# Order and waits of the DMA queue's loads where one Fourier layer ends and the next begins

## The reference, cut to what matters

```python
h = layer_norm(x @ fc0_w + fc0_b, ln0_g, ln0_b)
for i in range(4):
    x_ft = rfft2(h)
    out_ft[:, :, :12, :12]  = einsum('bixy,ioxy->boxy', x_ft[:, :, :12, :12],  w1[i])
    out_ft[:, :, -12:, :12] = einsum('bixy,ioxy->boxy', x_ft[:, :, -12:, :12], w2[i])
    h = layer_norm(irfft2(out_ft) + einsum('bchw,oc->bohw', h, conv_w[i]) + conv_b[i], ...)
    if i < 3: h = gelu(h)
```

## Time and profile before

| | |
|---|---|
| Runs | 3142.08, 3146.17 and 3292.08 us, median 3146.17 |
| Profiled execution | 3139.24 us |
| Its span, first to last instruction | 3137.6 us |
| PE busy | 2607.6 us (83%) |
| DVE / ACT / POOL busy | 65% / 52% / 21% |
| Mean granted clock of PE | 0.939 |
| Chain that ended last, by engine | PE 70%, DVE 13%, issue 6%, ACT 6%, DMA 4% |

### The profile page before, as it was taken

One profiled execution on the slowest core, in us unless ns is written; L12 is line 12 of the kernel. 1 busy time (PEld: TensorE's weight loads), 2 busy tenths in 40 slices (PEclk: granted clock), 3 DMA queues, 4 the chain that ended last, 5 costly groups with the idle time before them and its releaser, 6 DMA issues.

```text
span 3137.6 us, 82394 instructions
## 1 busy us (share of the span) xinstructions
PE 2607.6 (83%) x32240; PEld 1691.8 (54%) x32240; DVE 2033.2 (65%) x3091; ACT 1634.0 (52%) x1951; POOL 670.4 (21%) x402
## 2 busy tenths in 40 slices
PE   4677688899778899789899788999999969954994
PEld 2333356566556666566566543444444349952893
DVE  4888667788657788658888544555555452256557
ACT  4556444455335555335555346777777824422451
POOL 2332322323213232223322212311111110000000
PEclk9988999999989999999999898999999988986897
DMA  2523345745346755446655412241111000000000
GB/s 65 155 90 115 87 176 177 227 177 185 123 154 197 216 181 185 141 140 205 219 181 185 129 57 81 64 101 52 61 51 56 29 1 1 1 1 1 1 1 14
DMA packets 130762, 335.92 MB, mean 107 GB/s; under 512 B 66694, under 2 KB 94630, under 8 KB 94758
## 3 DMA queue, kind: packets, MB, share of 16 engines
q1 hardware_dynamic: 108070, 161.53, 16.7%
q10 hardware_dynamic: 18432, 134.23, 10.7%
q0 software_dynamic: 4096, 37.75, 5.5%
HBM read 179.30 MB, written 154.14 MB: 106 GB/s over the span
## 4 chain that ended last, share of the span: by engine, by line
PE 70%; DVE 13%; issue 6%; ACT 6%; DMA 4%; POOL 1%; SPq 1%; DVEq 0%; ACTq 0%; POOLq 0%
PE pA L1364 15%; PE pA L1374 8%; PE pT L1445 7%; PE pS L1416 6%; PE pT L1387 5%; PE pD L1434 4%; PE pD L462 4%; PE pA L462 3%; PE pD L1401 3%; ACT w_sb L1499 3%; DVE arena L1724 2%; PE pS L454 2%; PE pT L454 2%; PE pT L1459 2%; DVE h_rows L1714 2%
## 5 line engine op out<-in xcount | busy, mean ns | idle before, releaser
L1158 POOL TENSOR_TENSOR w_sb<-w_sb,small 128x1024 f32<-128x1024 f32 x320 | 608.4, 1915 | 1688.2 <-DVE small L208 1687.5
L1364 PEld LDWEIGHTS pA<-conv_bd,h_in 128*128 128x128 f32 x4096 | 496.8, 198 | 143.1 <-ACT w_sb L1499 65.1
L1364 PE MATMUL pA<-conv_bd,h_in 128*128 128x128 f32 x4096 | 535.8, 286 | 38.6 <-DMA h_in<-h_scratch 23.8
L1520 ACT ACTIVATE h_new<-pT,bet,gam 128x1024 f32<-128x1024 f32 x256 | 308.2, 1204 | 336.0 <-PE pT L1387 300.8
L1683 DVE TENSOR_REDUCE small<-arena 128x32 f32<-128x1056 f32 x320 | 390.0, 1219 | 138.4 <-ACT arena L1509 136.4
L1499 ACT COPY w_sb<-pA 128x1024 f32<-128x1024 f32 x256 | 258.9, 1011 | 328.1 <-PE pA L1374 280.1
L1387 PE MATMUL pT<-cst,w_sb 128*128 128x128 f32 x2048 | 291.0, 287 | 92.0 <-ACT h_new L1520 48.2
L1714 DVE STREAM_TRANSPOSE h_rows<-h_new 128x1024 f32<-128x1024 f32 x256 | 310.6, 1229 | 74.0 <-ACT h_new L1520 72.8
L1387 PEld LDWEIGHTS pT<-cst,w_sb 128*128 128x128 f32 x2048 | 229.3, 146 | 219.6 <-POOL w_sb L1158 95.1
L1509 ACT ACTIVATE arena<-w_sb 128x1024 f32<-128x1024 f32 x320 | 337.7, 1055 | 6.8 <-DVE w_sb L1676 2.7
L1374 PE MATMUL pA<-arena,cst 64*64 64x256 f32 x4096 | 282.7, 392 | 0.0
(11 more groups left out here) (299 smaller groups left out, 3594.0 us busy)
## 6 DMA issues: line engine op xcount, KB each, us to landing
h_scratch<-h_new ACTq DMA_DIRECT2D x128, 1024.0 KB, 4.2
h_in<-h_scratch SPq DMA_DIRECT2D x128, 1024.0 KB, 5.0
y_scratch<-w_sb POOLq DMA_DIRECT2D x32, 576.0 KB, 8.2
y_in<-y_scratch SPq DMA_DIRECT2D x512, 36.0 KB
w_sb<-in_L_tok_w1r_dram POOLq DMA_DIRECT2D x8, 576.0 KB, 6.7
w_sb<-in_L_tok_w1i_dram POOLq DMA_DIRECT2D x8, 576.0 KB, 6.9
w_sb<-in_L_tok_w2r_dram POOLq DMA_DIRECT2D x8, 576.0 KB, 6.5
w_sb<-in_L_tok_w2i_dram POOLq DMA_DIRECT2D x8, 576.0 KB, 6.6
```

What stands on the lines that cost most here:

```text
L1158: pool.tensor_tensor(z, z, r.broadcast_to([P, 32, C]), ALU.mult).then_inc(s["normed"], 1)
L1364: pe.matmul(pA[:, c:c + 128], h_in[:, 1024 * n + c:1024 * n + c + 128], conv_bd[:], start=(j == 0), stop=False, skip_group_check=True)
L1520: act.activation(h_new[:, 1024 * n:1024 * n + 1024], pT[:], ACT.Gelu if ph == "mid" else ACT.Identity, bias=bet[:, col], scale=gam[:, col] ...
```

## The change

`group` no longer waits for the stores of group 14. At the end of a middle layer the two `load_h(0, t)` wait only for `acc.1` and `acc.3` of group 15, as in any other group. At the end of the first stage they wait for the stores of the groups up to 7 alone. The wait for `y_stored` and `load_y(0)` move behind both `load_h`. One `alone` is added behind the first wait.

```diff
                 if not (end and ph == "last"):
                     p.sent(sp, op, p.ends(op)[1], g)
-                if end and ph != "last":
-                    y_is_stored(L if ph == "first" else L + 1, 0)
-                    load_y(0)
+                    if end:
+                        alone(sp)
+                if end and ph == "first":
                     for t in range(2):
-                        sp.wait_ge(s[f"stored{t}"], at("stored", ph, L, g, 0) + 16)
+                        sp.wait_ge(s[f"stored{t}"], at("stored", ph, L, NG // 2, 0) + 16)
                         alone(sp)
                 elif not end:
                     load_x(g + 1) if ph == "first" else load_y(g + 1)
...
                         load_h(0 if end else g + 1, t)
+                if end and ph != "last":
+                    y_is_stored(L if ph == "first" else L + 1, 0)
+                    load_y(0)
                 if then:
                     then()
```

## The result

The changed kernel takes 3115.77 us in the median, against 3144.12 before (8 runs each); the ratio is 0.9927, with a 95% interval from 0.9908 to 0.9946. The profiled execution took 3116.07 us with a span of 3114.4, 23.2 us less than the span before. So it is a gain of 0.7%: within the 2% that the forecast called no change, but the interval does not reach 1.

A forecast was written before the change was run, and what follows sets the result against it. PE carries the chain, with 23.8 us of waits for `h_in` behind SP's store wait. -29.5 + 1.5 + 3.0 = -25.0 us on 3139.24 gives 3114.2, plus 5 for the median: 3119 us, range 3106 to 3137.

The forecast's parts named there:

- The stall and its price: Three middle boundaries: PE's wait for the image before `acc.0` goes, saving 8.8, 9.8 and 10.9 us, 29.5 us in all.
- The body of 25.09 us: First boundary, from its `i1.0` to the next: 25.09 us, taken as the length of a body that waits for no image.
- the check against POOL: Fourth boundary: `turn.2-` needs POOL's scaling, done at 1787.6, so it starts then and not at 1798.56, 10.9 us saved.
- The small loads: Middle boundaries: the eight mixed-mode loads, moved behind the images, make `i1.0` late, 1.5 us in all; ends 0 and 14.
- 1.4 us to land: Small loads: last bytes moved at most 1.4 us after the last issue ended, when issued alone.
- the lower bound: Middle boundaries: eight small-load issues take 4.14 us, from some 854.9 to 859.1, land by 860.5 and cost nothing.
- the slower rival: Middle boundaries: small loads don't begin to issue until the 1 MB ahead has landed; 9.9 us late, 3160 us; 5% with anything slower.
- The first boundary: First boundary: image loads beside POOL's stores delay `y_stored` and the small loads, costing 3.0 us; ends 0 and 8.
- 0.66 MB, or 3.7 us, lost for each MB: First boundary, upper bound: POOL's stores lose this to each MB of image loads; two loads cost 7.3 us.
- the first rival: Small loads become the new wait at the middle boundaries, half the gain lost, 3137 us median; 18% including cases towards the forecast.
- The second: Rival: gain nearly whole at the middle boundaries, small-load and first-boundary costs both hidden, -29.5 us, 3114 us median; chance 12%.
- The fourth: Rival: another wait, such as `gelu.2-` for group 14's store, returns some 2 us at each boundary, 3125 us; chance 7%.

## Why the prediction was right, and where its steps were not

**The stall and its price: right.** The prediction had 8.8, 9.8 and 10.9 us for the three middle boundaries, 29.5 in all; the kernel with the store wait away and nothing else measured 9.0, 10.1 and 10.9, 30.0. The body of 25.09 us taken from the first boundary was the right yardstick (25.06 and 24.97), and the check against POOL at the fourth boundary was needed: `turn.2-` does wait for POOL there.

**The small loads: the term was too small.** I took 1.5 us for the three boundaries, and it measured 5.3. The step that failed is "1.4 us to land" behind a load that was to be over by 859.4. The issue was about as fast as the lower bound (4.33, 3.20 and 3.20 us against 4.14). With nothing ahead, `i1.0` starts 862.28 - 860.46 = 1.8 us behind the last issue; behind 1 MB it was 863.59 - 859.43 = 4.2 at the second boundary (3.7 and 3.3 at the others), behind 2 MB 858.76 - 852.58 = 6.2:

```profile
858.76 1.59 PE L1344 MATMUL pS<-y_in,cst 48*32 48x208 f32 x32 [5.45 <-DMA y_in<-y_scratch]
```

I had reckoned that the 1 MB would be out of the way by 859.4. It and the small loads share one queue: from 1309.5 to 1317 us of the changed kernel SP's queue (q1) carried both, and no other queue moved images or modes. The load of 1 MB itself, issued at 854.52 at the second boundary, took 7.3 us to land in place of 4.98, to 861.8, and 7.0 and 5.2 at the third and fourth; `i1.0` waited least where it landed soonest:

```profile
h_in<-h_scratch SPq DMA_DIRECT2D x1, 1024.0 KB, 7.3
...
q1 hardware_dynamic: 624, 1.34, 57.7%
h_in<-h_scratch SPq DMA_DIRECT2D x1, 1024.0 KB, 7.0
...
h_in<-h_scratch SPq DMA_DIRECT2D x1, 1024.0 KB, 5.2
```

The Trainium skill, "DMA: Bandwidth & Descriptors", section "Queues, rings and completion order", says that on each DMA engine the descriptors of a ring are consumed in order. The series from 0 to 2 MB agrees, and the rule was the right warning; the price I put on it was not. The same section says that data descriptors carry no barrier. That agrees as well: with 2 MB ahead, issued from 847.22 and landed 7.8 us after issue in the median, the small loads were issued from 848.27 to 852.58, so the slower rival's mechanism, an issue held until the images have landed, does not occur.

A second part of this cost is the clock, as in the stall that went away: over the 3 us from 863.5, right after the idle time, the granted clock of the changed kernel is 0.52, nearly all at the level of 1.2 GHz (0.50), and `i1.0` takes 1.59 us and not 0.91:

```profile
863.50:866.50 3.00, 2.91 (x39) 2.22 (x40) 1.23 (x2) 0.00 (x0) 0.00 (x0) 0.52 0.46 180
```

**The first boundary: the term was too large.** I took 3.0 us, and it was 0.2. POOL's stores and SP's image loads did run side by side. From 386 to 394 us, before (first row) only POOL's queue q0 moved images or modes, and after it POOL's q0 and SP's q1:

```profile
q0 software_dynamic: 213, 1.52, 83.3%
```

```profile
q0 software_dynamic: 207, 1.61, 56.0%
q1 hardware_dynamic: 196, 1.47, 44.1%
```

The stores moved as much in these 8 us as alone, and the loads 1.47 MB on top, but the lone stream had all but run out by 393 us. Up to 390 us, from 380.9, the stores had moved 1.72 MB before, and after it 1.45 MB beside 0.80 MB of loads:

```profile
q0 software_dynamic: 222, 1.72, 86.2%
```

```profile
q0 software_dynamic: 189, 1.45, 64.0%
q1 hardware_dynamic: 98, 0.80, 22.6%
```

So they do give way, by 0.27 MB for 0.80 MB, a third of a MB for each. The step that failed is the price, "0.66 MB, or 3.7 us, lost for each MB", taken from the earlier trace rows, where the other stream was a store to HBM; here it was a load from it. SP passed `y_stored` 15.2 us after POOL's first issue (380.94 to 396.14), not 12.9, so 2.3 us later and not 7.3, and the 4.3 us to spare at `i1.0` covered it. In the other runs with this order the delay was 1.5 to 4 us, and `i1.0` waited 0, 0.3, 0.56 or 1.31 us, so it is in part luck that nothing was left of the term in this run. Of the skill's rule that a DMA engine goes round between the queues packet by packet, the same section, the packets agree: 207 against 196. But my estimate by it, that the stores lose the time that the loads take, 5 us, doesn't hold here; and 5 us is near one load alone (4.98 us), while two take some 6.5 (2.0 MB from 867 to 873.5 us).

**The sum.** -29.5 + 1.5 + 3.0 = -25.0 became -24.7 + 0.2 = -24.5 at the boundaries: two errors of nearly 4 and 3 us with opposite signs. That the sum came out so close is luck. The span fell by 23.2. The rest is outside: near the end of the Fourier layers' MLP the lead is 26.5 us, two rows of the same matmuls before and after,

```profile
2478.98 1.93 PE L1459 MATMUL pT<-arena 128*32 128x256 f32 x32
```

```profile
2452.50 1.93 PE L1462 MATMUL pT<-arena 128*32 128x256 f32 x32
```

so some 2 us were won elsewhere, and 3.3 lost again in the token layers, which the change doesn't touch. Both lie with PE's clock. Of the 2 us, 1.6 are in the body that follows the second boundary's issue gap: there the tail's `turn` and `acc.0` ran at a granted clock of 0.62 before (first two rows) and at 1.00 after:

```profile
897.72 1.97 PE L1387 MATMUL pT<-cst,w_sb 128*128 128x128 f32 x8
899.48 2.72 PE L1364 MATMUL pA<-conv_bd,h_in 128*128 128x128 f32 x16
```

```profile
892.93 1.09 PE L1390 MATMUL pT<-cst,w_sb 128*128 128x128 f32 x8
893.86 1.95 PE L1367 MATMUL pA<-conv_bd,h_in 128*128 128x128 f32 x16
```

In the second run of the changed kernel the same two take 1.97 and 3.38 us, and with the small loads first 1.97 and 2.56, so this gain is chance and not the change's doing. From the two rows of the MLP to the end PE is busy 499.11 us before and 503.60 after with the same number of matmuls, at a mean granted clock of 0.86 and 0.85; that is enough for the 3.3 us.

**The signs.** The prediction wanted `i1.0` no more than 2 us behind `turn.0` at the middle boundaries: that held at the third and fourth (1.30 and 0.88 us), and the second, with 2.90 us, lies between the forecast's sign and the first rival's 3. The second boundary's 5.5 us is also just above the 5 below which the forecast was to be called wrong. `acc.0` had a gap at the fourth alone, 0.69 us, for DVE and not for a load.

**The rivals.** The first, small loads as the new wait, is what happened, at 5 us and not at 14. The second had the first boundary right. The third needs loads that are more than 10 us late; that was produced with the store waits kept, 14.5 us late, and was slower. The fourth, a store awaited elsewhere, did not show: no gelu waited at the boundary for the store of group 14.

## What to carry to other kernels

Where a queue waits for the youngest of something, ask which one the next step really needs; here the wait for stores 14 groups too young was worth 30 us over three layers, and all of the gain. Taking such a wait away needs no new order: what the engine wants first should stay first in the queue, and 1 MB ahead of small loads on the same queue made PE wait 0.9 to 2.9 us each time. When an order is moved, give each move its own run, since here one of the two edits paid for the other.

## What the runs showed that I had not expected

From 386 to 390 us POOL's stores alone kept the 16 DMA engines 95% busy at 221 GB/s, and beside image loads the same engines moved 352 GB/s at a share of 98% (last two numbers of each row, before and after):

```profile
386.00:390.00 4.00, 4.00 (x18) 1.98 (x16) 1.25 (x1) 2.23 (x2) 2.90 (x2) 0.61 0.95 221
```

```profile
386.00:390.00 4.00, 4.00 (x18) 2.10 (x16) 1.25 (x1) 2.07 (x2) 2.78 (x2) 0.60 0.98 352
```

So a busy share near full did not mean that nothing more would fit: the stores' own share of these 4 us fell from 95% to 56%, while what they moved fell only from 0.88 to 0.71 MB. Whether the small loads delay the 1 MB ahead of them as well is not shown: it took 7.3, 7.0 and 5.2 us to land at the three boundaries, and image loads of 1 MB there with nothing close behind them took from 4.8 to 6.3 us in these runs.
